# One multiplication for four query tiles in the output projection, and a row flag that is 1 or not-a-number

## The chip, the cores and the metric

The kernel runs on one core of one Trainium2 chip. The metric is the device time of one execution in microseconds (us). TensorE (PE) does matrix products and transposes, VectorE (DVE) elementwise work and reductions, ScalarE (ACT) activations and copies, GpSimd (POOL) the rest; SyncE (SP) issues transfers. The engines run side by side and wait for one another by semaphores only. Results of TensorE land in PSUM, in banks of 512 fp32 numbers in each of 128 partitions; everything else lies in SBUF.

## The reference, cut to what matters

Two layers, each an attention over a context of 1601 rows and then a feed-forward part with experts. The input x has 2048 rows of 256, the attention 16 heads of 16. Layer 0 is causal, layer 1 uses a mask and nothing else:

```
q = (layernorm(x) @ Wq.T + bq), k = (ctx @ Wk.T + bk), v = (ctx @ Wv.T + bv), split into 16 heads
scores = q k / sqrt(16); masked scores = -inf
attn   = softmax(scores) @ v          # sum of exp(s)*v divided by the sum of exp(s)
x      = x + tanh(g) * (attn @ Wo.T + bo)
```

A row of layer 1 whose scores are all masked comes out as not-a-number in the reference, since its softmax divides by nothing that is defined.

## The kernel before

The attention (function `attention`) leaves in the tile `OT` the numerators and, as a seventeenth value of each head, the denominator: the sum over the keys, with the query along the free axis. In layer 1 it also leaves `live`, 128 x 16 x 16, one number for each query row and head: 1 where the row's maximum is above -1e29, else 0. It is written in eleven pieces on VectorE, one for each unit of work (line 799). Attention of layer 1 exists twice in the program, for a mask that touches only the last keys (tiles that end in t) and for any mask (g); a branch picks one, and in the trace it is the first.

The function `output_projection` runs after it, in a block of its own; all engines meet at the block's ends. It works on four chunks c of 512 queries, each of four query tiles of 128, and inside a chunk on four head groups g of four heads: sixteen groups i = 4c + g.

- TensorE transposes four 128x128 pieces of `OT` into one of two PSUM banks (psA, line 885). Bank i % 2 is used again by group i, which waits until group i - 2 has been divided (`att_s`).
- VectorE waits for the transposes (`ot`) and makes the reciprocal of the 16 denominators of each partition in `rden`. In layer 0 this is one reciprocal (line 854). In layer 1 it is three instructions, each waiting for the one ahead (lines 846, 849, 852): times `live`, reciprocal, times `live`. A dead row gives 0, infinity and then 0 times infinity, which is not-a-number.
- VectorE then divides: four multiplications, one for each query tile, of 4 heads x 16 values by the group's reciprocals, from PSUM into `att` (line 858). Only the last one tells `att_s`.
- When the four groups of a chunk are divided, TensorE transposes `att` (line 897), ScalarE copies it to `aT` (line 873), and TensorE does 16 matmuls with Wo (line 910). VectorE adds the result to `xres` and gathers the statistics of the next layernorm (`residual`, lines 830 and 835).

TensorE's order is: groups of chunk 0, groups of chunk 1, then for each chunk its `att` transposes and matmuls, with the groups of the chunk after next behind them. VectorE's order is: the eight groups of chunks 0 and 1, residual 0, four groups, residual 1, four groups, residual 2, residual 3. All instructions of an engine run in the order of the program.

Of the kernel before, what the change touches and what calls it, by code (L numbers as in the profile page):

```python
# [12 lines left out]
ALU = mybir.AluOpType  # L13
# [3 lines left out]
P = 128  # L17
# [4 lines left out]
NQT = T // P  # L22
H = 16
DH = D // H
# [3 lines left out]
QTC = QC // P  # L28
# [11 lines left out]
G = 4  # L40
# [29 lines left out]
def build(nc, x_d, ctxT_d, mask_d, maskT_d, gx_d, gf_d, W, F, out_d):  # L70
    ctx = ExitStack()

    def sb(stack, name, shape, dt=F32):
        return stack.enter_context(nc.sbuf_tensor(name, shape, dt))
# [3 lines left out]
    def sem(name):  # L78
        layer_sems.append(nc.alloc_semaphore(name=name))
        return layer_sems[-1]  # L80
# [10 lines left out]
    with ctx:  # L91
# [5 lines left out]
        def bank(i):  # L97
            if i < AB:
                return psA[:, i, :]
            if i == AB:  # L100
                return psO[:, :]
            return psC[:, (i - 4) // 2, (i % 2) * 512:(i % 2) * 512 + 512]
# [331 lines left out]
        def attention(st, causal, masked, first, OT, live, Qs, tag, add_bias, beside=None, more=None):  # L434
# [88 lines left out]
            if masked:  # L523
                mrow = sb(st, f"mrow{tag}", [P, QTC, S], BF16)
                mcol = sb(st, f"mcol{tag}", [P, nt, QC], BF16)
                mi = sb(st, f"mi{tag}", [P, 2, QC], I32)
                mask_ld = [sem(f"a{tag}_mask_loaded{i}") for i in range(2)]
                mask_mk = sem(f"a{tag}_mask_made")
            ones_q = sb(st, f"ones_q{tag}", [1, P // 2], BF16)
            o_zero, q_ones, ones_made = sem(f"a{tag}_out_zeroed"), sem(f"a{tag}_q_ones"), sem(f"a{tag}_ones_made")  # L530
            q_ld = [sem(f"a{tag}_q_loaded{s}") for s in range(QN)]
# [240 lines left out]
            def vector(dve):  # L772

                dve.memset(psO[:, :], 0.0).then_inc(o_zero, 1)
                n = 0
                links = 0

                def link(ins):
                    nonlocal links
                    links += 1  # L780
                    ins.then_inc(chain, 1)
                    dve.wait_ge(chain, links)

                for u, (s, _, _) in enumerate(UNITS):
                    for n in range(n, max_end[u]):
                        _, h, (q, pc, k0, w, diag) = MAXIMA[n]
                        dve.wait_ge(a_done, n + 1)
                        dve.tensor_reduce(mxp[:, q, h, pc:pc + 1], psA[:, place_of[("piece", n)] % AB, 0:w],  # L788
                                          AX.X, ALU.max).then_inc(a_free, 1)
                    n = max_end[u]  # L790
                    h0, nh = heads[u][0], len(heads[u])
                    dve.wait_ge(a_free, n)
                    if u:
                        dve.wait_ge(m_tr, u)
                    m = mx[:, :, h0:h0 + nh]
                    p0, p1, p2 = (mparts[:, :, i * nh:(i + 1) * nh] for i in range(3))
                    link(dve.tensor_reduce(m, mxp[:, :, h0:h0 + nh, 0:len(PIECES[s]) // QTC], AX.X, ALU.max))
                    if live is not None:
                        link(dve.tensor_scalar(live[:, s * QTC:(s + 1) * QTC, h0:h0 + nh], m, DEAD, None, ALU.is_ge))
                    link(dve.tensor_scalar(p0, m, -1.0, None, ALU.mult))  # L800
                    link(dve.scalar_tensor_tensor(out=m, in0=m, scalar=-1.0, in1=p0, op0=ALU.mult, op1=ALU.subtract))
                    link(dve.tensor_scalar(p1, m, 1.0, None, ALU.mult))
                    link(dve.tensor_tensor(p2, m, p1, ALU.subtract))
                    dve.sem_inc(m_spl, 1)

            return sync, gpsimd, tensor, scalar, vector


        def output_projection(L, OT, live):
            NG = H // G  # L810
            with ExitStack() as st:
                w = W[L]
                att = sb(st, f"att{L}", [P, NQT, D])
# [3 lines left out]
                ld, chain, att_s = sem(f"o{L}_loaded"), sem(f"o{L}_chain"), sem(f"o{L}_att")  # L817
                ot, rd, stat = sem(f"o{L}_out_transposed"), sem(f"o{L}_sum_inverse"), sem(f"o{L}_stats")
                tr, tre, mm, up = (sem(f"o{L}_{n}") for n in ("transposed", "aT", "done", "residual"))
                with nc.Block() as block:  # L820
                    @block.sync
                    def _(sp):
                        sp.dma_start(wo[:, :, :], w["WoT"].rearrange("(k p) n -> p k n", p=P)).then_inc(ld, 16)
                    @block.vector
                    def _(dve):
                        def residual(g):
                            for i in (2 * g, 2 * g + 1):
                                dve.wait_ge(mm, i + 1)
                                v = xres[:, 2 * i:2 * i + 2, :].rearrange("p q d -> p (q d)")
                                dve.scalar_tensor_tensor(out=v, in0=bank(4 + i % 4), scalar=gates[:, L:L + 1], in1=v,  # L830
                                                         op0=ALU.mult, op1=ALU.add).then_inc(up, 1)
                                dve.wait_ge(up, i + 1)
                                for t in (2 * i, 2 * i + 1):

                                    dve.bn_stats(stats[:, t, :], xres[:, t, :]).then_inc(stat, 1)
                        nrd = 0
                        for c in range(NC):
                            for g in range(NG):
                                i = c * NG + g
                                dve.wait_ge(ot, i + 1)  # L840
                                o = bank(i % 2).rearrange("p (q u n) -> p q u n", q=QTC, u=G)
                                r = rden[:, i, :, :]
                                if live is not None:

                                    lv = live[:, c * QTC:(c + 1) * QTC, g * G:(g + 1) * G]
                                    dve.tensor_tensor(r, o[:, :, :, DH], lv, ALU.mult).then_inc(rd, 1)
                                    nrd += 1
                                    dve.wait_ge(rd, nrd)
                                    dve.reciprocal(r, r).then_inc(rd, 1)
                                    nrd += 1  # L850
                                    dve.wait_ge(rd, nrd)
                                    dve.tensor_tensor(r, r, lv, ALU.mult).then_inc(rd, 1)
                                else:
                                    dve.reciprocal(r, o[:, :, :, DH]).then_inc(rd, 1)
                                nrd += 1
                                dve.wait_ge(rd, nrd)
                                for q in range(QTC):
                                    last = dve.tensor_tensor(
                                        att[:, c * QTC + q, g * G * DH:(g + 1) * G * DH].rearrange("p (u d) -> p u d", u=G),
                                        o[:, q, :, 0:DH], r[:, q, :].unsqueeze(2).to_broadcast([P, G, DH]), ALU.mult)  # L860
                                last.then_inc(att_s, 1)
                            if c:
                                residual(c - 1)
                        residual(NC - 1)
# [124 lines left out]
        def attention_layer(L):  # L989
            with ExitStack() as st:  # L990
# [20 lines left out]
                if L == 0:  # L1011
                    with ExitStack() as at:
                        sync, gpsimd, tensor, scalar, vector = attention(at, True, False, 0, OT, None, Qs, "0",
                                                                          add_bias, count_masks(at), zero_rows)
                        with nc.Block() as block:
                            block.sync(sync)
                            block.gpsimd(gpsimd)
                            block.tensor(tensor)
                            block.scalar(scalar)
                            block.vector(vector)  # L1020
                else:

                    with ExitStack() as at:
                        tail = attention(at, False, False, TAIL, OT, live, Qs, "t", add_bias)
# [884 lines left out]
```

## Time and profile before

| | us |
|---|---|
| median of 3 runs | 1749.4 (1749.16 to 1749.73) |
| the profiled execution, its own time | 1748.56 |
| span of its trace | 1746.4 |
| output projection of layer 0, first transpose to end of last statistics | 540.3 to 577.4 |
| output projection of layer 1, the same | 1369.4 to 1411.9 |
| TensorE busy, share of the span | 84% |
| VectorE busy, share of the span | 50% |

The profiled execution is 0.8 us below the median and 2.2 us longer than its span. Times in rows count from the span's start. A row of the timeline merges instructions of one line that follow each other: its length is from the first start to the last end.

### The profile page before, as it was taken

What the parts mean: (1) busy time and instruction counts of PE and PEld (TensorE: products, weight loads), DVE (VectorE), ACT (ScalarE), POOL (GpSimd) and SP (SyncE); (2) the same over time, 40 slices, a digit from 0 to 9 for tenths busy, and PEclk for the clock granted to TensorE, in tenths of its full rate; (3) what the DMA queues carried; (4) which work ended last, traced back from release to release, by engine and by line L of the source; (5) the groups of instructions that cost most, each with busy time, mean ns of one, the idle gap of its engine ahead of it and who ended that gap; (6) DMA issues with size and microseconds to landing.
All of it is one profiled execution on the core that took longest, in us unless ns stands there. A gap on an engine that the chain in (4) does not pass through costs nothing. (4 is left out here: it accounts for less than half of the span.)

```text
span 1746.4 us, 25682 instructions
## 1 busy us (share of the span) xinstructions
PE 1474.8 (84%) x8697; PEld 898.7 (51%) x8698; DVE 873.3 (50%) x2084; ACT 672.9 (39%) x1100; POOL 362.9 (21%) x330
## 2 busy tenths in 40 slices
PE   4588999999898655999999997349999767999993
PEld 2333333333224534999999996212332453566662
DVE  4589898878744441222222222568886454211112
ACT  3223556667683111333333331215778321122221
POOL 0020000299900062000000000020000035234531
PEclk9879999999999667999999999668999877999997
DMA  3720303125230441027603201240110031124434
GB/s 112 254 65 20 111 19 110 39 95 186 76 95 7 171 169 50 24 93 216 157 24 101 95 23 45 79 148 18 30 30 3 8 125 40 53 79 143 145 98 155
DMA packets 98514, 153.29 MB, mean 88 GB/s; under 512 B 16769, under 2 KB 79419, under 8 KB 96255
## 3 DMA queue, kind: packets, MB, share of 16 engines
q1 hardware_dynamic: 66431, 90.48, 16.9%
q0 software_dynamic: 15232, 45.99, 7.8%
q10 hardware_dynamic: 16768, 15.77, 3.0%
q8 instruction: 45, 0.74, 0.2%
q14 instruction: 38, 0.31, 0.1%
HBM read 108.05 MB, written 47.69 MB: 89 GB/s over the span
## 5 line engine op out<-in xcount | busy, mean ns | idle before, releaser
L788 DVE TENSOR_REDUCE mxp<-psA 128x1 f32<-128x384 f32 (+4 forms) x640 | 334.8, 577 | 66.6 <-PE psA L644 47.2
L762 ACT ACTIVATE Pt<-psC 128x1024 f32<-128x1024 f32 (+4 forms) x296 | 256.2, 918 | 158.1 <-PE psC L670 82.7
L644 PE MATMUL psA<-Kst,Qst 97*128 97x384 bf16 (+4 forms) x640 | 182.9, 352 | 34.6 <-DVE mxp L788 18.9
L1343 PE MATMUL psA<-xTt,w 128*128 128x128 f32 x1728 | 202.6, 278 | 4.3 <-issue 4.1
L1343 PEld LDWEIGHTS psA<-xTt,w 128*128 128x128 f32 x1728 | 197.7, 193 | 10.7 <-issue 10.7
L788 DVE TENSOR_REDUCE mxpt<-psA 128x1 f32<-128x449 f32 x256 | 145.2, 619 | 34.8 <-PE psA L644 29.4
L670 PE MATMUL psC<-Qst,Kst 100*128 100x512 bf16 (+4 forms) x592 | 152.1, 361 | 0.7 <-ACT Pt L762 0.2
L644 PEld LDWEIGHTS psA<-Kst,Qst 97*128 97x128 bf16 x640 | 55.5, 100 | 180.5 <-DVE mxp L788 131.2
L1431 DVE SCALAR_TENSOR_TENSOR hT<-psA,b,sil 128x128 f32<-128x128 f32 x216 | 64.2, 345 | 167.0 <-ACT sil L1406 166.9
L762 ACT ACTIVATE Ptt<-psC 128x1024 f32<-128x1024 f32 (+1 forms) x128 | 123.8, 1020 | 47.6 <-PE psC L670 47.2
L693 PE MATMUL psO<-Pt,Vaug 128*17 128x512 f32 (+4 forms) x1184 | 141.8, 550 | 0.0
L1352 PE MATMUL psC<-w,hT 128*128 x576 | 127.3, 379 | 0.0
L1352 PEld LDWEIGHTS psC<-w,hT 128*128 128x128 f32 x576 | 108.0, 190 | 13.9
L1296 POOL DMA_INDIRECT outs<-yv,lab x36 | 35.4, 982 | 375.6 <-DVE yv L1443 375.6
L644 PE MATMUL psA<-Kst,Qstt 97*128 97x449 bf16 x256 | 83.5, 392 | 29.3 <-DMA Qstt<-q_parts 22.3
L1406 ACT ACTIVATE sil<-psA,b 128x128 f32<-128x128 f32 x216 | 65.6, 364 | 83.9 <-PE psA L1343 83.6
L670 PEld LDWEIGHTS psC<-Qst,Kst 100*128 100x128 bf16 (+1 forms) x592 | 55.3, 100 | 61.6 <-ACT Pt L762 19.6
L1085 POOL DMA_INDIRECT rows<-fxn,slot x64 | 71.4, 1116 | 23.6 <-issue 19.4
L1406 ACT ACT_TABLE_LOAD x18 | 23.1, 1283 | 136.9 <-PE psA L1343 136.9
L644 PEld LDWEIGHTS psA<-Kst,Qstt 97*128 97x128 bf16 x256 | 21.6, 100 | 103.3 <-DVE mxpt L788 60.1
L1691 DVE TENSOR_TENSOR hT<-sil,psA 128x320 f32<-128x320 f32 (+1 forms) x24 | 11.7, 487 | 122.3 <-ACT sil L1643 112.3
L1343 PE MATMUL psO<-xTt,w 128*128 128x128 f32 x576 | 70.2, 275 | 0.0
(279 smaller groups left out, 2016.4 us busy)
## 6 DMA issues: line engine op xcount, KB each, us to landing
w<-L_w SPq DMA_DIRECT2D x8, 2048.0 KB
mi<-mask POOLq DMA_DIRECT2D x16, 800.5 KB
rows<-blank SPq DMA_DIRECT2D x7, 1419.0 KB, 8.4
Kst<-k_parts SPq DMA_DIRECT2D x12, 800.5 KB, 15.9
w<-L_w SPq DMA_DIRECT2D x8, 1024.0 KB
q_parts<-parts ACTq DMA_DIRECT2D x4, 1536.0 KB, 15.0
Qst<-q_parts SPq DMA_DIRECT2D x48, 128.0 KB, 3.1
Qstt<-q_parts SPq DMA_DIRECT2D x48, 128.0 KB, 2.9
```

The source lines that it names most:

```text
L644: mmi = pe.matmul(out, Qst[0:KA, half[u] % QN, at:at + P], Kst[0:KA, h, k0:k0 + w], start=True, stop=diag is None and not masked)
L670: mmi = pe.matmul(psC[0:kw, n % 2, y * 512 + col:y * 512 + QC], Kst[0:KC, h, k0:k0 + kw], Qst[0:KC, half[u] % QN, at + col:at + QC], start ...
L693: mmi = pe.matmul(psO[32 * c:32 * c + NV, col:QC], Vaug[0:kw, first + j, g * G + c, :], Pt[0:kw, n % SLOTS, y, col:QC], start=(j == 0), st ...
L762: act.activation(Pt[0:kw, n % SLOTS, :, col:QC], psC[0:kw, n % 2, :].rearrange("p (y t) -> p y t", y=2)[:, :, col:QC], ACT.Exp).then_inc(p ...
L788: dve.tensor_reduce(mxp[:, q, h, pc:pc + 1], psA[:, place_of[("piece", n)] % AB, 0:w], AX.X, ALU.max).then_inc(a_free, 1)
L1085: pool.indirect_dma_start(xs[:, :], bass.IndirectOffsetOnAxis(ap=slot[:, k, t:t + 1], axis=0), xn[:, t, :], None, bounds_check=ROWS - 1, o ...
L1296: pool.indirect_dma_start(ys[:, :], bass.IndirectOffsetOnAxis(ap=lab[:, z, 0:1].bitcast(U32), axis=0), yv[:, z, :], None, bounds_check=2 * ...
L1343: mmi = pe.matmul(bank(j)[:, i * P:(i + 1) * P], w1[:, side, k, f * P:(f + 1) * P], xTt[:, z, k, :], start=(k == 0), stop=(k == KD - 1))
L1352: mmi = pe.matmul(bank(4 + z)[:, 0:D], hT[:, z, f * P:(f + 1) * P], w2[:, bass.ds(odd * (NF * D) + f * D, D)], start=(f == 0), stop=(f == ...
L1406: last = act.activation(sil[:, j, i, :], bank(j)[:, i * P:(i + 1) * P], ACT.Silu, bias=b1[:, bass.ds(e * (2 * NF) + (2 * j + i), 1)])
L1431: last = dve.scalar_tensor_tensor(out=hT[:, z, f * P:(f + 1) * P], in0=bank(j)[:, (2 + i) * P:(3 + i) * P], scalar=b1[:, bass.ds(e * (2 * ...
L1691: dve.tensor_tensor(hT1[0:fw, q % 2, m, 0:CAP], sil[0:fw, b, 0:CAP], bank(2 * b + 1)[0:fw, 0:CAP], ALU.mult).then_inc(h, 1)
```

## The change

The four multiplications of a group become one instruction over all four query tiles (a 4 x 4 x 16 pattern of 256 numbers in each partition; the reciprocals are repeated along the last axis). In layer 1 the first of the three steps towards the reciprocal is gone: reciprocal of the denominators straight from PSUM, then times `live`. So that a dead row still becomes not-a-number, the attention, once it has written all of `live`, takes the reciprocal of `live` and multiplies it by `live`: 1 stays 1, and 0 becomes 0 times infinity. These two instructions work on 256 numbers in each partition and stand behind all units of VectorE's program in that block, in both copies of the attention of layer 1; one of the copies is executed.

```
--- before.py
+++ after.py
@@ attention @@
+            if live is not None:
+                live_inv = sb(st, f"live_inv{tag}", [P, NQT, H])
...
                     link(dve.tensor_tensor(p2, m, p1, ALU.subtract))
                     dve.sem_inc(m_spl, 1)
+                if live is not None:
+
+                    link(dve.reciprocal(live_inv[:, :, :], live[:, :, :]))
+                    link(dve.tensor_tensor(live[:, :, :], live[:, :, :], live_inv[:, :, :], ALU.mult))
@@ output_projection @@
                                     lv = live[:, c * QTC:(c + 1) * QTC, g * G:(g + 1) * G]
-                                    dve.tensor_tensor(r, o[:, :, :, DH], lv, ALU.mult).then_inc(rd, 1)
-                                    nrd += 1
-                                    dve.wait_ge(rd, nrd)
-                                    dve.reciprocal(r, r).then_inc(rd, 1)
+                                    dve.reciprocal(r, o[:, :, :, DH]).then_inc(rd, 1)
                                     nrd += 1
                                     dve.wait_ge(rd, nrd)
                                     dve.tensor_tensor(r, r, lv, ALU.mult).then_inc(rd, 1)
...
-                                for q in range(QTC):
-                                    last = dve.tensor_tensor(
-                                        att[:, c * QTC + q, g * G * DH:(g + 1) * G * DH].rearrange("p (u d) -> p u d", u=G),
-                                        o[:, q, :, 0:DH], r[:, q, :].unsqueeze(2).to_broadcast([P, G, DH]), ALU.mult)
-                                last.then_inc(att_s, 1)
+                                dve.tensor_tensor(
+                                    att[:, c * QTC:(c + 1) * QTC, g * G * DH:(g + 1) * G * DH]
+                                    .rearrange("p q (u d) -> p q u d", u=G),
+                                    o[:, :, :, 0:DH], r.unsqueeze(3).to_broadcast([P, QTC, G, DH]), ALU.mult).then_inc(att_s, 1)
```

On TensorE, ScalarE, GpSimd and SyncE the instructions and their order stay as they were. On VectorE the projection of layer 1 reads as follows before, for the first two groups (rden holds the reciprocals, psA is the group's bank):

```order
 L846 TENSOR_TENSOR rden<-psA,live 128x16
 L849 RECIPROCAL rden<-rden 128x16
 L852 TENSOR_TENSOR rden<-rden,live 128x16
 L858 TENSOR_TENSOR att<-psA,rden 128x64 x4
 L846 TENSOR_TENSOR rden<-psA,live 128x16
```

and with the change, the end of the attention's block (the copy that stands last) included:

```order
 L805 TENSOR_TENSOR mpartsg<-mxg,mpartsg 128x4x4
 L809 RECIPROCAL live_invg<-live 128x256
 L810 TENSOR_TENSOR live<-live,live_invg 128x256
 L1035 UNCONDITIONAL_BRANCH
 L830 UNCONDITIONAL_BRANCH
 L852 RECIPROCAL rden<-psA 128x16
 L855 TENSOR_TENSOR rden<-rden,live 128x16
 L860 TENSOR_TENSOR att<-psA,rden 128x4x64
```

Seven instructions of a group in layer 1 have become three, and two have come ahead of the block's end. In layer 0 five have become two.

## Rows read from the trace of the kernel before

**Rows 1.** Page, busy time of each engine, share of span and instructions.

```profile
PE 1474.8 (84%) x8697; PEld 898.7 (51%) x8698; DVE 873.3 (50%) x2084; ACT 672.9 (39%) x1100; POOL 362.9 (21%) x330
```

**Rows 2.** Timeline, layer 0, start: start, length, engine, line, tiles, count, [idle before <-releaser].

```profile
540.27 1.07 PE L885 MATMUL psA<-ident,OT 128*128 128x128 f32 x8 [0.95 <-PEq L1015]
540.93 0.26 DVE L854 RECIPROCAL rden<-psA 128x16 f32<-128x16 f32 x1 [37.01 <-PE psA L885]
541.23 0.62 DVE L858 TENSOR_TENSOR att<-psA,rden 128x64 f32<-128x64 f32 x4
...
541.90 0.66 PE L885 MATMUL psA<-ident,OT 128*128 128x128 f32 x4 [0.57 <-DVE att L858]
...
542.60 0.26 DVE L854 RECIPROCAL rden<-psA 128x16 f32<-128x16 f32 x1
```

**Rows 3.** Timeline, layer 0, groups 5 and 7 and the first transposes of att.

```profile
545.09 0.25 DVE L854 RECIPROCAL rden<-psA 128x16 f32<-128x16 f32 x1
...
546.04 0.66 PE L885 MATMUL psA<-ident,OT 128*128 128x128 f32 x4 [0.16 <-DVE att L858]
...
546.53 0.60 PE L897 MATMUL psA<-ident,att 128*128 128x128 f32 x4
```

**Rows 4.** Timeline, layer 0, chunk 2: groups 8 to 11.

```profile
552.85 0.75 DVE L835 BATCH_NORM_STATS2 stats<-xres 128x6 f32<-128x256 f32 x2
553.52 0.24 DVE L854 RECIPROCAL rden<-psA 128x16 f32<-128x16 f32 x1
...
555.29 0.66 PE L885 MATMUL psA<-ident,OT 128*128 128x128 f32 x4 [0.16 <-DVE att L858]
```

**Rows 5.** Timeline, layer 1, start.

```profile
1369.40 1.77 PE L885 MATMUL psA<-ident,OT 128*128 128x128 f32 x8 [2.98 <-PEq L1036]
1370.36 0.17 DVE L846 TENSOR_TENSOR rden<-psA,live 128x16 f32<-128x16 f32 x1 [20.38 <-PE psA L885]
...
1371.07 0.62 DVE L858 TENSOR_TENSOR att<-psA,rden 128x64 f32<-128x64 f32 x4
...
1371.74 2.35 PE L885 MATMUL psA<-ident,OT 128*128 128x128 f32 x8 [0.56 <-DVE att L858]
...
1372.89 0.17 DVE L846 TENSOR_TENSOR rden<-psA,live 128x16 f32<-128x16 f32 x1
```

**Rows 6.** Timeline, layer 1: weight loads of group 7's transposes; first output matmuls.

```profile
1378.04 0.71 PEld L885 LDWEIGHTS psA<-ident,OT 128*128 128x128 f32 x4 [0.52 <-DVE att L858]
...
1381.16 3.72 PE L910 MATMUL psC<-wo,aT 128*128 128x256 f32 x16 [0.74 <-ACT aT L873]
```

**Rows 7.** Timeline, layer 1, chunk 2: group 8 starts, group 11's transposes start.

```profile
1386.38 0.16 DVE L846 TENSOR_TENSOR rden<-psA,live 128x16 f32<-128x16 f32 x1
...
1388.97 0.66 PE L885 MATMUL psA<-ident,OT 128*128 128x128 f32 x4 [0.57 <-DVE att L858]
```

**Rows 8.** Groups of VectorE by line and shape: busy us, mean ns, idle before.

```profile
L858 DVE TENSOR_TENSOR att<-psA,rden 128x64 f32<-128x64 f32 x128 | 19.8, 217 | 1.1
...
L422 DVE TENSOR_TENSOR Vaug<-psC,bvb 128x256 f32<-128x256 f32 x12 | 5.1, 424 | 6.5 <-PE psC L361 6.2 <-DVE parts L409 0.3
...
L849 DVE RECIPROCAL rden<-rden 128x16 f32<-128x16 f32 x16 | 4.0, 253 | 0.5
```

**Rows 9.** Stretches (length, PE, PEld, DVE, ACT, POOL busy, clock, DMA); then router matmuls.

```profile
591.00:604.00 13.00, 12.63 (x62) 12.53 (x61) 0.30 (x2) 0.71 (x1) 0.00 (x0) 0.51 0.77 268
...
1421.00:1427.00 6.00, 4.92 (x40) 4.12 (x39) 0.98 (x3) 4.15 (x6) 6.00 (x10) 1.00 1.03 351
...
1369.40:1379.00 9.60, 8.31 (x33) 5.91 (x34) 7.92 (x48) 0.00 (x0) 0.00 (x0) 0.51 0.08 28
...
1380.00:1381.00 1.00, 0.43 (x4) 0.19 (x2) 0.52 (x4) 0.97 (x2) 0.00 (x0) 1.00 0.00 0
...
L1168 PE MATMUL psA<-wr,fxT 128*128 128x8 f32 x64 | 13.1, 349 | 0.8 <-ACT fxT L1144 0.8
...
L1168 PE MATMUL psA<-wr,fxT 128*128 128x16 f32 x64 | 10.9, 324 | 0.8 <-ACT fxT L1144 0.8
```

## The prediction

> **What bounds the kernel now.** I read the page's busy times first: TensorE is busy 84% of the span, VectorE 50% [rows 1]. That average says nothing of the stage that is changed, so I went to the timeline of the two output projections, where both engines work in turns. The reader should follow one bank of PSUM round its loop. In layer 0 the reciprocal of group 0 starts at 540.93, its four multiplications at 541.23; they end at 541.85, and 0.05 us later, at 541.90, TensorE starts the transposes of group 2 into the freed bank. These take 0.66, and at 542.60 the reciprocal of group 2 starts [rows 2]. The loop is 0.30 + 0.62 + 0.05 + 0.66 + 0.04 = 1.67 us for the two groups that the two banks carry. VectorE by itself needs 0.30 + 0.53 = 0.83 for a group (the next reciprocal starts before the last multiplication's record ends), so the loop and the engine are about equally late. The division is on the path: TensorE's transposes of group 7 wait for group 5's division, and TensorE cannot begin the transposes of att ahead of them [rows 3].
>
> The same holds later in each layer, in a shorter form. In chunk 2 VectorE comes out of the statistics at 553.5 and does groups 8 and 9; the transposes of group 11 start at 555.29, when group 9 is divided, and the att transposes, ScalarE's copy and the 16 matmuls of chunk 1 stand behind them [rows 4]. Chunk 3 repeats this. So of the 16 divisions of a layer eight lie on the path: groups 0, 1, 3, 5 at the start, 8 and 9, 12 and 13. The others lie beside TensorE's work. In layer 1 the path is the same with three small instructions ahead of each division: 1370.36 to 1371.07 is 0.71 where layer 0 has 0.30, and the loop for two groups was 2.53 (1370.36 to 1372.89) with TensorE at half clock [rows 5, 9].
>
> **The division.** It removes four instructions of 64 numbers and adds one of 256. Four took 0.62 from first start to last end [rows 2], at 217 ns each [rows 8], so a start every 0.135. For the one, the nearest row is another TENSOR_TENSOR of the same engine on 128x256 fp32 numbers from PSUM with an output in pieces of 16, line 422: 424 ns [rows 8]. Between the two rows lie 192 numbers and 207 ns, about one number per ns, so most of what is saved is the fixed part of three instructions. I take 0.42 and save 0.20 each. Where the next instruction follows without a wait, the spacing counts: the statistics, also 256 numbers, stand 0.33 apart (0.75 for two of about 0.42) [rows 4], against 0.53 now, again 0.20. The ends of the unknown: 0.41 if the fixed part shrinks a little, and 0.62 if the longer pattern runs as slowly as four short ones, which is a rival below. The new loop of layer 0 is 0.30 + 0.42 + 0.05 + 0.66 + 0.04 = 1.47; VectorE needs 0.63 a group and TensorE about 0.53 to 0.66, so the loop sets the pace, and no other engine becomes late next. Gain in layer 0: 8 x 0.20 = 1.6 us. In layer 1: the same 8 x 0.20 = 1.6.
>
> The Trainium skill, in "VectorE: DVE Perf Modes", section "The TRN2 errata — SBUF-src ops pay a fixed extra latency per instruction", says that the latency is exposed between instructions, so that many small tiles pay it each. Here four small ones overlap, 0.62 and not 4 x 217 ns [rows 2, 8]; the trace contradicts the strong form. Its cycle figure for PSUM to SBUF, 120 cycles plus one for each number at 0.96 GHz, would be an estimate of 0.39 us for the long instruction; with 0.62 as measured for the four, sixteen of them would give 0.5 us more in all.
>
> **The step towards the reciprocal.** Layer 1 loses one multiplication of 16 numbers and its wait. Start of line 846 to start of the division is 0.71; two of the three steps remain, and layer 0's reciprocal from PSUM takes 0.30 with its wait [rows 2]. Three steps in 0.71 with one of about 0.29 leave 0.21 for each multiplication. Groups on the path: the same eight. Gain 8 x 0.21 = 1.7 us. Check on chunk 2: now group 8 starts at 1386.38 and group 11's transposes at 1388.97, 2.59 later [rows 7]; new, 0.83 until group 9 starts (0.50 + 0.33), then 0.50 + 0.42 + 0.05 = 0.97, together 1.80, a gain of 0.79, against 2 x 0.41 = 0.82 by the count. At the start of the layer TensorE has half clock: the first eight transposes took 1.77 there and 1.07 in layer 0 [rows 2, 5]. Its loop then is 2.53 - 0.41 = 2.12, still longer than TensorE's own two turns (about 1.8), so the gain is not swallowed there.
>
> **The two instructions on `live`.** They stand at the end of the attention's block on VectorE. VectorE has nothing after its last unit until the projection: 20.38 us idle, released by the projection's own first transposes [rows 5]. The multiplication of 256 numbers is 0.42 by the same row. The reciprocal of 16 numbers takes 253 ns, about 80 more than a multiplication of 16; the extra is either fixed, giving 0.5 us, or goes with the count, 16 times 80 ns more, giving 1.7. With waits 1 to 2.2 us, hidden by 20.38. Cost nothing; a cost only appears above some 16 us, as the other engines end the block about 3 us ahead of the projection. The extra waits of this chain have nothing queued behind them on VectorE but the block's end.
>
> **The clock.** In layer 1 TensorE had a gap of 2.98 us ahead of the projection [rows 5], and then ran with a granted clock of 0.51 from 1369.4 to 1379, and 1.00 from 1380 on [rows 9]: 1.2 and 2.4 GHz. The first output matmuls started at 1381.16 [rows 6], 11.8 us after the first transpose, with the full clock there about 10.5 after it. With 1.6 us less ahead of them they start about 10.1 after. If the clock rises at the same distance from the start, four transposes more run at half (0.35, from 1.77 against 1.07 for eight) and 0.4 us of matmuls (0.2). If the denser work lets it rise earlier, this costs nothing. Between 0 and 0.55; I take 0.25.
>
> **The sum.** 1.6 (layer 0) + 1.6 + 1.7 (layer 1) = 4.9, by the more exact loops 4.84, less 0.25: 4.6 us. The profiled execution would go from 1748.56 to 1744.0, with a span near 1741.8; the median, 0.8 above it, from 1749.4 to **1744.8**. Everything after a projection starts behind a meeting of all engines and issues its transfers there, so I expect the shift to be handed on whole.
>
> **Rivals.**
>
> *The clock comes out otherwise further on, with either sign.* Router matmuls: 64 took 13.1 us in layer 0 and 10.9 in layer 1. In layer 0 nearly all ran at 0.51; in layer 1 the first part, until 1427, ran at 1.00 [rows 9]. So where the change from full to half falls on a stretch of narrow matmuls is worth up to 2.2 us, once in each layer, and an earlier arrival of this stage moves it against that change. If the fall does not move with the work, layer 0's router gains: about 1.6 us more of it at full clock, which replaces twice as much at half, 1.6. A further 1.4 is to be had if layer 1's projection no longer starts at half (the loop of two groups would be 1.68 and not 2.12, three times). Kinder: 1.4 to 3.5 more, 1741.3 to 1743.4, chance 0.20. Less kind: 1.6 to 4 of the gain lost in later stages, 1746.4 to 1748.8, chance 0.14. Against both: most executions stand within 0.6 us of each other.
>
> The Trainium skill, in "TensorE: Matmul & The Clock Gate", Part 4, says that a transpose does not count as TensorE work for the clock. In the trace the clock rose by 1380 when TensorE had done nothing but transposes since 1369.4, so the row speaks against it. By that rule the first matmuls would start at half and chunk 0's could cost up to 3.7 us more, leaving a gain of about 1 (1748.5). I count it in the less kind case, with 0.04 of its chance.
>
> *The long multiplication is no cheaper than four short ones.* Its pattern has three axes and a repeated operand. Then only the removed step pays: 8 x 0.21 = 1.7, 1747.7. Against it: the 424 ns of line 422, whose output also is in pieces of 16. Chance 0.04.
>
> *Slower.* One mechanism: the full clock does not come in layer 1's projection at all, as the output matmuls come with transposes and waits in between. Each batch of 16 takes 3.72 at full clock [rows 6] and would take about 7.4; four batches cost 14.8 and the time is 1749.4 - 4.8 + 14.8 = 1759. It is slower than 0.2% from some 8.3 us of such loss, over two batches' worth. Against it: the rise came within 10.6 us during sparser work. Chance 0.03.
>
> *It does not do what it says:* the chain turns out to be paced by TensorE even so, and the 0.20 of groups 0, 1, 3, 5 shrinks by half; that is inside the forecast's own range.
>
> **How the numbers follow.** Forecast, 3.1 to 6.0 us gained, 1743.4 to 1746.3: 0.59. Faster by over 0.2% (about what a measurement of this kernel can tell from no change) means below 1745.9: 0.20 of the kinder case, 0.51 of the forecast's 0.59: 0.71. Within 0.2%: the rest, 0.26. Slower: 0.03. The range 1741.6 to 1747.2 leaves out the far ends of both clock cases, most of the third rival and the slower one, together some 0.17.
>
> **What would show it right or wrong.** Line 860 at 0.42 us, 32 times, and line 858 gone; a loop of 1.47 in layer 0; group 8 to group 11's transposes 1.37 in layer 0 (1.77 now) and 1.80 in layer 1; lines 809 and 810 well ahead of the block's end; VectorE's busy time down. First transpose to last statistics: 37.1 to 35.5 in layer 0, 42.5 to 39.5 in layer 1. Wrong would be: those two lengths as said and the time not, which would put the difference on the clock further on; or line 860 at 0.6.

## The result and the profile after

| | before | after |
|---|---|---|
| median of 20 runs, us | 1747.72 | 1740.95 |
| ratio after / before | | 0.9969 (0.9954 to 0.9984) |
| the profiled execution / its span | 1748.56 / 1746.4 | 1742.14 / 1740.1 |
| length of the projection of layer 0 | 37.16 | 35.60 |
| length of the projection of layer 1 | 42.54 | 38.71 |

The length of a projection is here always from its first transpose to the end of its last statistics. Single runs of one kernel spread over 15 us, and the ratio is not the quotient of the two medians (that would be 0.9961) but agrees with that of the two means, 1741.19 and 1746.52. The ratio applied to the median that stood before the prediction, 1749.4, gives 1744.0, 0.8 us from the forecast of 1744.8. A second measurement of the same changed kernel gave 0.9958 (0.9943 to 0.9973). The change made the kernel faster by 0.3 to 0.4%.

The timeline of the changed kernel at the start of layer 0 answers [rows 2, 3]. The columns are as there; lines from 858 on have new numbers, the long multiplication is line 860.

```profile
540.85 0.26 DVE L857 RECIPROCAL rden<-psA 128x16 f32<-128x16 f32 x1 [37.00 <-PE psA L887]
541.14 0.42 DVE L860 TENSOR_TENSOR att<-psA,rden 128x256 f32<-128x256 f32 x1
541.48 0.25 DVE L857 RECIPROCAL rden<-psA 128x16 f32<-128x16 f32 x1
...
541.62 1.27 PE L887 MATMUL psA<-ident,OT 128*128 128x128 f32 x8 [0.37 <-DVE att L860]
...
542.61 0.42 DVE L860 TENSOR_TENSOR att<-psA,rden 128x256 f32<-128x256 f32 x1
```

Group 0's division starts at 541.14 and group 2's at 542.61: the loop is 1.47 us, as worked out, where it was 1.67. TensorE restarts 0.06 after the 0.42 of the division. The same engine at the start of layer 1, against [rows 5, 6]:

```profile
1368.36 1.07 PE L887 MATMUL psA<-ident,OT 128*128 128x128 f32 x8 [2.96 <-PEq L1038]
1369.03 0.26 DVE L852 RECIPROCAL rden<-psA 128x16 f32<-128x16 f32 x1 [17.71 <-PE psA L887]
...
1369.53 0.42 DVE L860 TENSOR_TENSOR att<-psA,rden 128x256 f32<-128x256 f32 x1
...
1370.01 1.97 PE L887 MATMUL psA<-ident,OT 128*128 128x128 f32 x8 [0.58 <-DVE att L860]
...
1377.89 3.72 PE L912 MATMUL psC<-wo,aT 128*128 128x256 f32 x16 [0.74 <-ACT aT L875]
```

The way to the division is 0.50 (1369.03 to 1369.53) and was 0.71. At half clock the loop of one bank is now 2.14 us (reciprocals at 1371.16 and 1373.30), 2.12 forecast; TensorE is busy for 1.97 of it, where the prediction had about 1.8 for its two turns, and VectorE now waits 0.36 for it in each. The first output matmuls come 9.53 us after the first transpose and came 11.76 after it. And the groups of VectorE by line and shape, against [rows 8] (busy us, mean ns, idle before):

```profile
L860 DVE TENSOR_TENSOR att<-psA,rden 128x256 f32<-128x256 f32 x32 | 13.6, 424 | 1.1
L852 DVE RECIPROCAL rden<-psA 128x16 f32<-128x16 f32 x16 | 4.0, 252 | 18.8 <-PE psA L887 18.8
...
L809 DVE RECIPROCAL live_invt<-live 128x256 f32<-128x256 f32 x1 | 1.8, 1753 | 0.1
L810 DVE TENSOR_TENSOR live<-live,live_invt 128x256 f32<-128x256 f32 x1 | 0.4, 425 | 0.0
```

The long multiplication takes 424 ns, the mean of line 422 to the nanosecond. From the start of group 8 to the transposes of group 11 it is 1.37 us in layer 0 and 1.79 in layer 1 (1.37 and 1.80 forecast), and VectorE's busy time went from 873.3 to 867.0 us.

### The profile page after: what moved, and what is told of

It reads as the page before. It is cut to its first block and busy times, and to the rows that moved or that the text cites. A ratio compares the mean times of both kernels' runs of the same rounds, so it can differ in the third digit from the quotient of the medians.

```text
span 1740.1 us, 25572 instructions
## 1 busy us (share of the span) xinstructions
PE 1473.5 (85%) x8697; PEld 897.7 (52%) x8698; DVE 867.0 (50%) x1974; ACT 673.5 (39%) x1100; POOL 362.8 (21%) x330
## 5 line engine op out<-in xcount | busy, mean ns | idle before, releaser
L1345 PEld LDWEIGHTS psA<-xTt,w 128*128 128x128 f32 x1728 | 198.7, 194 | 10.9 <-issue 10.9
```

The costliest lines, as they stand in the source:

```text
L1345: mmi = pe.matmul(bank(j)[:, i * P:(i + 1) * P], w1[:, side, k, f * P:(f + 1) * P], xTt[:, z, k, :], start=(k == 0), stop=(k == KD - 1))
```

## The experiments

A ruler that serves all of them is the distance from one batch of output matmuls to the next, chunk 0 to 1 and 1 to 2: it holds what groups 8, 9, 12 and 13 and the statistics ahead of them do to the path, and at full clock it repeats to 0.01 us. What the first groups do to it stands in another distance, from the first transpose to the first output matmuls. Before it is 9.24 and 9.25 in layer 0, 10.08 and 10.07 in layer 1; after, 8.85 and 8.86, 9.28 and 9.27.

**The long multiplication alone.**

```
-                                for q in range(QTC):
-                                    last = dve.tensor_tensor(att[:, c * QTC + q, ...], o[:, q, :, 0:DH], ...)
-                                last.then_inc(att_s, 1)
+                                dve.tensor_tensor(att[:, c * QTC:(c + 1) * QTC, ...], o[:, :, :, 0:DH], ...).then_inc(att_s, 1)
```

> The one multiplication over four query tiles, with the three steps towards the reciprocal as before. Lengths are from the first transpose of a projection to the end of its last statistics (before: 37.2 us in layer 0, 42.5 in layer 1; with the whole change: 35.6 and 38.7). My theory, eight divisions of sixteen on the path at 0.20 us each: 35.6 in layer 0, 40.9 in layer 1, 3.2 us less in all. Rival, every one of the sixteen divisions counts: 34.0 and 39.3. Rival, only the shorter chain pays: 37.2 and 42.5.

Layer 0 was 35.60 long, as expected. Layer 1 was 42.88, nothing like 40.9, though its first output matmuls came 9.98 after the first transpose (11.76 before). TensorE's batches of layer 1 in this run's timeline:

```profile
1378.09 3.72 PE L909 MATMUL psC<-wo,aT 128*128 128x256 f32 x16 [0.74 <-ACT aT L872]
1388.34 6.06 PE L909 MATMUL psC<-wo,aT 128*128 128x256 f32 x16 [0.69 <-ACT aT L872]
1400.36 3.72 PE L909 MATMUL psC<-wo,aT 128*128 128x256 f32 x16 [0.74 <-ACT aT L872]
```

and three stretches of it (length, busy us of PE, PEld, DVE, ACT, POOL, granted clock, DMA share and GB/s):

```profile
1378.00:1386.00 8.00, 5.74 (x32) 4.80 (x33) 5.34 (x17) 0.04 (x1) 0.00 (x0) 1.00 0.00 0
1387.00:1393.00 6.00, 5.31 (x15) 4.02 (x14) 1.30 (x4) 1.03 (x2) 0.00 (x0) 0.50 0.01 3
1394.00:1404.00 10.00, 7.09 (x43) 5.83 (x42) 6.73 (x22) 1.09 (x2) 0.00 (x0) 1.00 0.00 0
```

In the middle of the projection the clock fell from 2.4 to 1.2 GHz and came back. The batch that it met took 6.06 in place of 3.72, the distances became 10.25 and 12.02 where about 9.68 each was due (10.07 less the 0.39 that the long multiplication gave in layer 0); 2.9 us in all. It fell after a stretch in which TensorE was busy 5.74 of 8 us, with a wait for VectorE in it. That this is the reason is not shown: in the kernel before, the same stretch of layer 1 (1381.07 to 1389.07) has TensorE busy for 5.35 of 8 us only, and no fall followed. The time, 0.9995 (0.9978 to 1.0012) in 12 runs, can be told neither from the expectation of 0.998 nor from no change.

**The shorter chain alone**, the other part of the diff, with four multiplications as before.

> The shorter way to the reciprocal and the two instructions on the row flag, with four multiplications as before. My theory, eight multiplications of 16 numbers on the path at 0.21 us: layer 0 stays 37.2, layer 1 goes from 42.5 to 40.9, 1.7 us less in all, and the two instructions on the flag cost nothing. Rival, all sixteen count: 39.1 in layer 1. Rival, the loop at half clock is paced by TensorE at the start: 41.6.

Layer 0: 37.13, nothing gained, right. Layer 1: 42.35, and again one fall of the clock, here too in the second batch, 2.9 us by the distances (10.32 and 11.90 where 9.66 was due):

```profile
1380.32 3.72 PE L913 MATMUL psC<-wo,aT 128*128 128x256 f32 x16 [0.74 <-ACT aT L876]
1390.64 5.95 PE L913 MATMUL psC<-wo,aT 128*128 128x256 f32 x16 [0.69 <-ACT aT L876]
1402.54 3.72 PE L913 MATMUL psC<-wo,aT 128*128 128x256 f32 x16 [0.74 <-ACT aT L876]
```

The first output matmuls came 9.51 after the first transpose, with a shorter piece at half clock at the start than in the kernel before (about 3.6 us in place of 10.2). Ratio 0.998 (0.9958 to 1.0002) in 12 runs, 0.999 expected. The lengths of layer 1 in these two runs could not decide between eight and sixteen; the next two could.

**Which divisions are on the path.** In both runs the whole change is in, but one half of the groups keeps four multiplications.

```
+                                if i in (0, 1, 3, 5, 8, 9, 12, 13):      # the other run: if i not in (...)
                                     dve.tensor_tensor(att[:, c * QTC:(c + 1) * QTC, ...]   # one
+                                else:
+                                    for q in range(QTC): ...                               # four
```

> The whole change, but only groups 0, 1, 3, 5, 8, 9, 12 and 13 get the one multiplication; the other eight keep four. My theory, these eight are the path: all of the gain, 35.6 to 35.8 us in layer 0 and 38.7 to 39.1 in layer 1. Rival, each of the sixteen gives its share: half of it, 36.4 in layer 0 and 39.8 in layer 1.

> The whole change, but only groups 2, 4, 6, 7, 10, 11, 14 and 15 get the one multiplication; the eight that I hold to be the path keep four. My theory: none of the joining's gain, 37.2 us in layer 0 and 40.9 in layer 1 (the shorter chain alone). Rival, each gives its share: 36.4 and 39.8.

Batches of layer 0 with the eight groups of my path joined:

```profile
548.71 3.72 PE L919 MATMUL psC<-wo,aT 128*128 128x256 f32 x16 [0.74 <-ACT aT L882]
557.57 3.72 PE L919 MATMUL psC<-wo,aT 128*128 128x256 f32 x16 [0.74 <-ACT aT L882]
566.43 3.72 PE L919 MATMUL psC<-wo,aT 128*128 128x256 f32 x16 [0.74 <-ACT aT L882]
```

The distances are 8.86 and 8.86, in layer 1 9.28 and 9.27: all of the gain of chunks 2 and 3 comes from groups 8, 9, 12, 13, and joining 10, 11, 14 and 15 adds nothing. With the other eight joined, layer 1's one distance at full clock was 9.66, which is 10.07 less the shorter chain and none of the division. For these chunks the theory stands and the rival (each gives its share) falls.

For the start it was incomplete. With 0, 1, 3, 5 joined the first output matmuls of layer 0 came 7.64 after the first transpose; 8.04 before, 7.27 with all. Only half of the 0.77 was there. The timeline of that run shows why:

```profile
543.20 0.26 DVE L857 RECIPROCAL rden<-psA 128x16 f32<-128x16 f32 x1
543.49 0.61 DVE L867 TENSOR_TENSOR att<-psA,rden 128x64 f32<-128x64 f32 x4
...
544.16 1.28 PE L894 MATMUL psA<-ident,OT 128*128 128x128 f32 x8 [0.38 <-DVE att L867]
544.30 0.42 DVE L861 TENSOR_TENSOR att<-psA,rden 128x256 f32<-128x256 f32 x1
...
544.85 0.26 DVE L857 RECIPROCAL rden<-psA 128x16 f32<-128x16 f32 x1
```

Group 2, still with four, keeps the loop of its own bank at 1.65 (543.20 to 544.85), and group 5 stands behind group 4 on VectorE, so the short loop of the other bank waits for the long one. With 2, 4, 6, 7 joined and 1, 3, 5 not, it was 8.02, no gain. Both loops must be short. With the whole change they are, and the sum was right. That groups 2 and 4 make up the rest, and not 6 and 7, follows from the order of the program (6 and 7 are divided behind 5, and the last transposes of the start wait for 5); no run joined 0 to 5 alone. So the length of layer 0 was 35.98 in the first of the two runs, above the 35.6 to 35.8 expected; layer 1's was 38.29, below the 38.7 to 39.1, with only some 3.4 us at half clock at its start.

The second of the two runs also met the fall of the clock in layer 0 (a batch of 5.96, length 40.03), and in layer 1 the half clock of the start lasted until the first batch, which took 5.64 (length 43.35). Its lengths therefore do not test the 37.2 and 40.9 that were expected; the 8.02 and the 9.66 do.

**The changed kernel again.**

> The changed kernel once more, unaltered. Theory: the lengths of the two projections where TensorE has its full clock repeat to 0.1 us (35.6 us in layer 0; from first output matmuls to the next 8.85 in layer 0 and 9.28 in layer 1), and what differs between executions is where the clock changes: time and mean granted clock move together. Rival: the executions differ in something else (transfers), and the clock's changes stand at the same places as in the first trace. Ratio to before 0.997.

Length 35.60 in layer 0, distances 8.86, 8.85, 9.28, 9.27. Layer 1 was 37.91 and not 38.71, all of the difference ahead of the first output matmuls (8.72 and not 9.53), where the clock was 0.80 on average and not 0.57. The stretch from 1368.3 to 1376.0 in the first trace of the changed kernel, columns as above:

```profile
1368.30:1376.00 7.70, 6.73 (x32) 5.34 (x33) 5.40 (x21) 0.00 (x0) 0.00 (x0) 0.57 0.14 38
```

and the same stretch in this one:

```profile
1368.30:1376.00 7.70, 6.42 (x37) 4.53 (x35) 6.35 (x24) 0.80 (x2) 0.00 (x0) 0.80 0.12 35
```

The 64 router matmuls of layer 1 took 10.0 us in the first trace and 13.0 in this one, those of layer 0 12.1 and 12.9. Over the 20 runs of the changed kernel, time and mean granted clock go together (correlation -0.89), with 1732.7 us at a clock of 0.920 and 1747.7 at 0.911. The places where the clock changes are not the same in each execution of one program. It is not shown that they make all of the difference: outside the two projections the two traces took 1665.8 and 1665.0 us although layer 1's router matmuls stand 3.0 us apart the other way, and transfers were not compared. In the eight runs of this measurement, which spread over 5 us only, the correlation is weak (-0.21).

**TensorE's waits filled.**

```
+                                if c >= 2 and g == 2:
+                                    for _ in range(8):
+                                        pe.transpose(bank(2)[:, 0:P], OT[:, 0:P], ident[:, :])
```

> The changed kernel with eight more transposes (results not used) on TensorE in chunks 2 and 3 of each projection, where it waits 1.4 to 1.6 us for the division of group 8 or 12. Eight take 1.04 us, so they fit the wait and cost nothing by themselves. Theory: the drop to half clock in the middle of a projection, seen in three of the traces so far and worth 2.5 to 3 us each, comes when TensorE waits much there; with the gaps filled it does not come, the lengths stay 35.6 and about 38.7, and the median is 1 to 2 us under the changed kernel's. Rival: transposes do not keep the clock up; nothing changes. Rival: they delay group 10 and cost 4 x 0.3 = 1 us.

The eight transposes cost nothing: distances 8.85, 8.85, 9.28, 9.27, lengths 35.60 and 38.63. No fall came, but none had come in the changed kernel's traces without them either, and the ratio of 0.9963 (0.9947 to 0.9979) lies between the two of the changed kernel. The median, expected 1 to 2 us under the changed kernel's, was 1 us above it (1741.14 against 1740.10 measured beside it). Whether they keep the clock up is open; the run told nothing apart.

**Twelve more reciprocals of the flag.**

```
-                    link(dve.reciprocal(live_inv[:, :, :], live[:, :, :]))
+                    for _ in range(13):
+                        link(dve.reciprocal(live_inv[:, :, :], live[:, :, :]))
```

> The changed kernel with the reciprocal of the row flag taken thirteen times in place of once. In the changed kernel's trace it takes 1.75 us (1.79 with its wait) and VectorE ends at 1351.3, where ScalarE's last copy of the attention ends at 1366.04 and the projection's first transpose starts 2.32 us after that. Theory, hidden until some 14.7 us and then paid in full: twelve more are 21.5 us, VectorE ends 6.7 us behind ScalarE, and the first transpose comes 9.0 us after ScalarE's last copy. Rival, VectorE's work there is waited for by something earlier: more than 9.0, up to 23.8. Rival, the block's end does not wait for VectorE: 2.3.

VectorE and ScalarE and then the first transpose of layer 1:

```profile
1349.24 23.20 DVE L810 RECIPROCAL live_invt<-live 128x256 f32<-128x256 f32 x13
1365.58 0.60 ACT L751 ACTIVATE OT<-psO 128x512 f32<-128x512 f32 x1 [1.14 <-PE psO L695]
1372.48 0.43 DVE L811 TENSOR_TENSOR live<-live,live_invt 128x256 f32<-128x256 f32 x1
1376.13 1.94 PE L888 MATMUL psA<-ident,OT 128*128 128x128 f32 x8 [10.60 <-PEq L1039]
```

The first transpose came 9.95 after ScalarE's last copy, 9.0 expected. The cover is real: about 14 us more than the one reciprocal with its multiplication (2.2 us, until 1351.3), 16 in all, and those two sit well inside. The 0.95 that was not expected: from VectorE's end to the first transpose it is 3.22, from ScalarE's it was 2.32 (2.3 to 2.65 in the other traces). This run also had a fall of the clock in layer 1 (a batch of 6.10), with the whole change in.

**The kernel before, two more traces.**

> The kernel before once more, unaltered. Theory: where VectorE makes TensorE wait longest in a projection (9.24 us from output matmuls to output matmuls in layer 0, 10.08 in layer 1), the clock falls to half in some executions, and one such fall costs 2.4 to 3 us; in the traces so far it came in 4 of 7 projections with the old division or the old chain and in none of 13 with the whole change. Expected of two projections: one with a fall. Rival: the fall comes with the experiments' other orders and not in the kernel before: none.

> The kernel before once more, as in the run ahead, with the same expectation: a fall to half clock inside the middle of one of its two projections, or none by the rival. Without a fall the spacings are 9.24 and 10.08 us.

The first of the two had the fall, in layer 0, in the third batch; the second had none and repeated 9.24, 9.24, 10.07 and 10.07:

```profile
548.21 3.72 PE L910 MATMUL psC<-wo,aT 128*128 128x256 f32 x16 [0.74 <-ACT aT L873]
557.46 3.72 PE L910 MATMUL psC<-wo,aT 128*128 128x256 f32 x16 [0.74 <-ACT aT L873]
567.38 5.93 PE L910 MATMUL psC<-wo,aT 128*128 128x256 f32 x16 [0.69 <-ACT aT L873]
574.93 3.72 PE L910 MATMUL psC<-wo,aT 128*128 128x256 f32 x16 [0.74 <-ACT aT L873]
```

Its layer 0 was 40.84 long; 0.8 of that lies ahead of the first output matmuls (8.83 and not 8.04), with a piece of about 3.4 us at half clock there. So the kernel before has these falls too; it is not the experiments' order that makes them. One fall in the four projections of the two traces is less than the one in two expected, and it came in layer 0, where TensorE's waits are the shorter ones.

**A half of the residual behind the groups.**

```
-                        def residual(g):
-                            for i in (2 * g, 2 * g + 1):
+                        def residual(g, halves=(0, 1)):
+                            for i in (2 * g + z for z in halves):
...
                             if c:
-                                residual(c - 1)
-                        residual(NC - 1)
+                                if c >= 2:
+                                    residual(c - 2, (1,))
+                                residual(c - 1, (0,))
+                        residual(NC - 2, (1,))
+                        residual(NC - 1)
```

> The changed kernel with VectorE's program in another order: after the first half of a chunk's residual come the four groups of the chunk after next, then the second half. Group 8 (12) then starts when its transposes are there and not when all statistics are done, 1.05 us earlier, twice in each layer. Theory: from output matmuls to output matmuls 8.85 becomes 7.8 in layer 0 and 9.28 becomes 8.2 in layer 1; lengths 33.5 and 36.5; 4.2 us less than the changed kernel, 0.994 to 0.995 of the kernel before. Rival: the second half, now later, delays the matmuls that need its PSUM bank or the end of the layer: no gain.

Distances 7.86 and 7.86 in layer 0, 8.27 and 8.28 in layer 1; lengths 33.60 and 36.47. Ratio to before 0.9935 (0.9916 to 0.9954) in 6 runs. By lengths the two projections are 4.2 us shorter than in the first trace of the changed kernel, as expected. The theory stands, the rival falls.

**Two groups ahead of the output matmuls.** On top of the halves, TensorE transposes groups 8, 9 (12, 13) while ScalarE copies, and groups 10, 11 (14, 15) right behind the batch. VectorE's order, not shown here, is: groups 0 to 9, first half of residual 0, groups 10 to 13, its second half, first half of residual 1, groups 14 and 15, its second half, and the rest.

```
+                            if g and 4 * g + 6 < NC * NG:
+                                heads_back(range(4 * g + 6, 4 * g + 8))
                             pe.wait_ge(att_s, NG * (g + 1))
                             ...                                      # transposes of att
+                            if 4 * g + 8 < NC * NG:
+                                heads_back(range(4 * g + 8, 4 * g + 10))
                             pe.wait_ge(tre, 2 * (g + 1))
```

> The changed kernel with another order on TensorE and VectorE: two of the four groups of a coming chunk are transposed while ScalarE copies the att transposes (ahead of the output matmuls), and divided during the matmuls; the other two stand behind the matmuls, and TensorE needs no wait for VectorE there. The residual is in halves as in the run before. Theory: from output matmuls to output matmuls 6.3 us in layer 0 (8.85 now) and 6.65 in layer 1 (9.28 now), twice each, and 0.3 later at the start: lengths 30.8 and 33.9, 9.6 us less than the changed kernel, 0.991 to 0.992 of the kernel before. Rival: the two pairs wait for each other across the two banks and only the gain of the halves stays, 33.5 and 36.5.

```profile
547.54 3.72 PE L919 MATMUL psC<-wo,aT 128*128 128x256 f32 x16
553.75 3.72 PE L919 MATMUL psC<-wo,aT 128*128 128x256 f32 x16
559.95 3.72 PE L919 MATMUL psC<-wo,aT 128*128 128x256 f32 x16 [0.74 <-ACT aT L880]
```

These are the batches of layer 0. What stands on TensorE between the first two, from the same timeline:

```profile
551.10 1.04 PE L892 MATMUL psA<-ident,OT 128*128 128x128 f32 x8
...
551.97 0.60 PE L904 MATMUL psA<-ident,att 128*128 128x128 f32 x4
...
552.84 1.04 PE L892 MATMUL psA<-ident,OT 128*128 128x128 f32 x8
```

The first two batches have no wait of TensorE ahead of them any more, and the att transposes stand directly behind the group transposes. Distances 6.21 and 6.20 in layer 0, 6.50 and 6.10 in layer 1, somewhat under the 6.3 and 6.65 expected; lengths 30.30 and 32.69, under the 30.8 and 33.9. The 0.3 us that was expected on top at the start did not come (7.26 to the first output matmuls of layer 0, 7.27 in the changed kernel). Ratio to before 0.9895 (0.9872 to 0.9918) in 6 runs: 1% less than the kernel before and the fastest of all. It changes nothing in what is computed.

## Why the prediction was right, point by point

**What bounds.** Right where it says that the division is on the path. The list of eight divisions was right for chunks 2 and 3, as the two split runs show to 0.01 us. For the start the list 0, 1, 3, 5 was too short: those four alone gave 0.40 of the 0.77 us. The loops of both banks have to shrink, so 2 and 4 belong to it by the order of the program. The sum did not suffer, since the change shortens all and the gain of the start is the same four steps of 0.20 either way; that the number held there is luck as far as the list goes, and the step would have misled whoever changed only those four.

**The division.** 0.42 forecast, 424 ns measured; loop 1.47 forecast and measured. Gain of layer 0: 1.6 forecast, 37.16 to 35.60 measured.

**The step towards the reciprocal.** 0.71 to 0.50, as forecast. Distances of layer 1: 0.79 to 0.82 forecast, 0.80 measured. The loop at half clock: 2.12 forecast, 2.14 measured.

**The two instructions on the flag.** Cost nothing, as forecast; the reciprocal of 256 numbers took 1.75, so its price goes with the count (1.7 was the upper end). The cover ends at about 14 us beyond these two, which with their 2.2 is the 16 that was written.

**The clock at the start of layer 1.** This term of the sum had the wrong sign. I took 0.25 us as lost; instead the first output matmuls came 2.23 us earlier after the first transpose (3.04 in the second trace), where the path alone gives about 1.6. What failed is the assumption that the full clock comes at a fixed distance from the first transpose.

By the granted clock, read in steps of 0.2 us, the half clock lasted from 0.2 to 10.4 us after the first transpose in the trace of before; in the two of after from 1.0 to 7.8 (so the first eight transposes took 1.07 and not 1.77) and from 0.4 to 3.8. The first output matmuls came after 9.53 and 8.72 us with the change (9.45, 9.30, 9.46, 9.11 and 9.02 in the variants that keep it or its eight divisions), after 11.76, 11.69 and 12.30 before. That is 0.6 to 1.4 us against the first trace which the sum did not have, the lower part of what the kinder case priced. It is not owed to the whole change: the shorter chain alone had 9.51, with the half clock from 0.4 to 4.0, and the long multiplication alone 9.98, where half of the path's gain would give about 10.9 to each. And it is not sure with most of it: the run with the other eight joined had half clock until 15.4 and 11.48. So layer 1 was 38.71 and 37.91 long where 39.5 was forecast. Why the half clock mostly ends sooner is not shown; that the transposes stand closer together is a guess.

**The total.** Sum of the path 4.84. The lengths of both projections in three traces of before and two of after: 79.7, 83.3 and 80.2 us against 74.3 and 73.5. Measured over all runs: 0.31 and 0.42% of 1748 us, 5.4 and 7.3 us. The forecast of 4.6 is inside the first interval (2.8 to 8.0) and just short of the second (4.7 to 10.0). What lies beyond the path inside the projections is clock: the start of layer 1, and falls in the middle. In the profiled pair the spans differ by 6.3 us: 5.4 in the two lengths, 0.9 outside them. What is outside the projections took 1666.7, 1667.4 and 1667.3 us in the three traces of before and 1665.8 and 1665.0 in the two of after, so no part of the gain was lost outside them, as forecast. But over all traces it lies between 1660.7 and 1670.8 (the delay of 7.6 us by the twelve reciprocals taken off). That spread is wider than the effect, and no run says where it arises.

The time forecast, 1744.8, started from 1749.4, which three runs gave; the median of twenty is 1747.7. So the gain is the number to compare (4.6 against 5.4 and 7.3), and of the 3.9 us by which the median after, 1740.95, lies under the forecast, 1.7 come from that start.

**Falls in the middle.** The prediction did not see them: it looked at one trace of before, in which there was none. A fall in the middle came in 4 of 11 projections with the old division or the old chain (before 1 of 6, the chain alone 1 of 2, the long multiplication alone 1 in layer 1, the other eight 1 of 2, whose second had the half clock of the start reach into its first batch), and in 1 of 15 with the path shortened as the change does or more. My expectation of none with the whole change was wrong by that one. The picture that fewer waits of TensorE mean fewer falls has these counts for it and two things against it: the run that was to show it by filling the waits showed nothing, and the projection with the longest waits, layer 1 of the kernel before (TensorE busy 5.35 of the 8 us from its first batch on, a wait of 1.98 in them), had no fall in any of three traces, while the five falls came behind stretches with 5.74 to 6.2 of 8. It is open.

**The rivals.** Further on the clock did come out otherwise, with both signs: router matmuls between 10.0 and 13.1 us in the same or the other layer. But the three traces of the kernel before have the same range (13.1, 11.2 and 10.1 in layer 0), so nothing here ties it to the change. What the prediction set against both clock cases, that executions stand within 0.6 us of each other, was wrong: twenty spread over 15. The slower case did not come: the output batches ran at full clock in layer 1 once the start was over, and in both traces of the changed kernel the first of them took 3.72, so the case in which it starts at half did not come either; it did in the run with the other eight joined (5.64). The long multiplication was cheaper than four short ones (0.42 against 0.62), and the start was not paced by TensorE (0.77 gained in layer 0, 0.8 forecast).

## What to carry to other kernels

Where two engines hand banks to each other, write the loop of one bank as a sum of rows (work, handover, work, handover) and compare it with each engine's own turn; the longest sets the pace, and an engine that runs in program order couples the loops, so an edit must shorten all of them. Then look what stands ahead of the engine that is waited for: here its order (statistics ahead of a division that TensorE was waiting for) was worth 4.2 us in the two lengths, and the new order of both engines on top of it another 7.1, against 5 for the instructions themselves. When executions of one program spread by more than the effect, measure it as a distance inside the trace between two events at full clock: 0.2 us could be read to 0.01 where medians of 12 runs could not place 1.7.

## What the runs showed of the hardware that I had not expected

- Executions of one program differ in where TensorE's clock changes. The changed kernel spread from 1732.7 to 1747.7 us in 20 runs, the kernel before from 1737.5 to 1752.4; that the three runs shown before the prediction agree within 0.6 us was luck.
- TensorE fell to 1.2 GHz in the middle of a stretch in which it was busy 5.74 of 8 us, with one wait of 1.79 us for VectorE in it; it did not fall in three other executions after it had been busy 5.35 of 8 with a wait of 1.98. One fall lengthened a batch of 16 matmuls from 3.72 to about 6 us and the projection by about 3.
- A reciprocal on VectorE costs about 1.75 us for 256 fp32 numbers in each partition where a multiplication costs 0.42; with 16 numbers it is 0.25 against 0.17. Between these two sizes it is paid for each number, not once.
- After VectorE as the last engine the next block began 3.22 us later (one trace), after ScalarE 2.3 to 2.65. The cause is open.
